# Experts' output rows scattered to their picks' places, and the combine stage regrouped, in a fused four-layer graph kernel

## The reference, cut to what matters

```python
x = _layernorm(x + _L3_gnn_ref(x, ...))          # x is [3125, 256], float32
# inside _L3_gnn_ref
x = m @ W_gc + b_gc + (feats @ W_res + b_res)    # "X4" in the kernel
vals, idx = top_k(x @ Wg + bg, 2); gates = softmax(vals)
h1 = gelu(rows_of_expert @ w1[e] + b1[e])        # 256 -> 512
h2 = h1 @ w2[e] + b2[e]                          # 512 -> 256
y = x + sum over the two picks of gate * h2[row]
out = (y - mean(y, 0)) * rsqrt(var(y, 0) + eps) * gamma + beta
```

## Time and profile before

| | |
|---|---|
| median of 3 runs | 2125.81 us (2124.03 to 2128.05) |
| the profiled execution's own time | 2125.8 us |
| its span | 2124.1 us |
| mean granted TensorE clock | 0.939 of full speed |
| busy share of the span | PE 86%, DVE 43%, ACT 22%, POOL 18% |
| moved by DMA | 553.6 MB, mean 261 GB/s |

### The profile page before, as it was taken

How to read it: one execution, slowest core, us unless ns; L and a number is a source line. 1 busy time by engine, 2 the same in 40 slices (tenths; PEclk the granted TensorE clock), 3 DMA queues, 4 the chain that set the end, 5 groups by cost and what they waited for, 6 DMA issues and landing times. The chain is left out here.

```text
span 2124.1 us, 34378 instructions
## 1 busy us (share of the span) xinstructions
PE 1819.4 (86%) x9586; PEld 1445.4 (68%) x9620; DVE 907.9 (43%) x2788; ACT 466.9 (22%) x1245; POOL 390.2 (18%) x723
## 2 busy tenths in 40 slices
PE   1988885999899899999989999899993999999451
PEld 0355554788688788777778878688882888888220
DVE  4976664444434411122211157736665121222256
ACT  0034444322222211111111111111110332232010
POOL 1022223311111200000000012214443111111451
PEclk8999997999999999999999999999996999999656
DMA  4178999999588688766668889889973999999421
GB/s 123 31 249 305 324 324 348 315 321 326 183 294 264 201 271 288 260 216 215 215 214 289 289 275 289 266 269 307 309 250 131 327 372 369 359 373 371 160 71 60
DMA packets 284900, 553.57 MB, mean 261 GB/s; under 512 B 17170, under 2 KB 208328, under 8 KB 281608
## 3 DMA queue, kind: packets, MB, share of 16 engines
q1 hardware_dynamic: 275976, 528.36, 75.1%
q0 software_dynamic: 8832, 24.13, 3.3%
HBM read 415.14 MB, written 137.29 MB: 260 GB/s over the span
## 5 line engine op out<-in xcount | busy, mean ns | idle before, releaser
L1001 PE MATMUL psum<-xsa,blk 128*128 128x512 f32 x2500 | 639.3, 405 | 18.1 <-DVEq L356 8.2
L1001 PEld LDWEIGHTS psum<-xsa,blk 128*128 128x128 f32 x2500 | 462.4, 191 | 106.5 <-issue 10.7
L1001 PE MATMUL psum<-xsb,blk 128*128 128x512 f32 (+1 forms) x1875 | 416.2, 369 | 6.0 <-DVEq L356 5.9
L1001 PEld LDWEIGHTS psum<-xsb,blk 128*128 128x128 f32 x1875 | 321.6, 190 | 64.8 <-issue 7.0
L1360 DVE TENSOR_SCALAR onehots<-counts_scratch 128x348 bf16<-128x348 f16 x464 | 161.6, 374 | 79.9 <-issue 41.5
L903 PE MATMUL psum<-onehots 128*128 128x349 bf16 x464 | 146.7, 316 | 40.8 <-DVE onehots L1365 38.5
L509 PE MATMUL psum<-route,expert_weights 128*128 128x128 f32 x1360 | 169.0, 278 | 0.0
L1759 POOL TENSOR_SCALAR ve<-mv 128x1 f32<-128x1 f32 x75 | 16.8, 223 | 820.5 <-DVE mv L1475 820.5
L906 PE MATMUL psum<-zrow 128*128 128x512 bf16 x431 | 160.8, 381 | 0.0
L509 PEld LDWEIGHTS psum<-route,expert_weights 128*128 128x128 f32 x1360 | 159.8, 193 | 0.9
L519 PE MATMUL psum<-expert_weights,route 128*128 128x256 f32 x672 | 159.1, 380 | 0.6 <-ACT route L568 0.6
(11 more groups left out here) (299 smaller groups left out, 2076.8 us busy)
## 6 DMA issues: line engine op xcount, KB each, us to landing
blk<-counts_src_on_rows SPq DMA_DIRECT2D x125, 832.0 KB, 4.7
blk<-counts_src_on_rows SPq DMA_DIRECT2D x125, 768.0 KB
expert_weights<-in_L_gnn_w SPq DMA_DIRECT2D x176, 512.0 KB, 6.1
blk<-counts_dst_on_rows SPq DMA_DIRECT2D x50, 832.0 KB, 4.5
counts_dst_on_rows<-band_rows SPq DMA_DIRECT2D x25, 1600.0 KB, 8.4
blk<-counts_dst_on_rows SPq DMA_DIRECT2D x50, 768.0 KB
counts_src_on_rows<-blk SPq DMA_DIRECT2D x13, 1600.0 KB, 8.6
counts_src_on_rows<-rblk SPq DMA_DIRECT2D x12, 1600.0 KB, 9.7
```

The lines of the kernel that those rows point to most:

```text
L1001: mm = e.matmul(o, blk[n][:, k * P:(k + 1) * P], XS[:, k, :, 0:Fw], start=(k == 0), stop=(k == T - 1 and not own))
```

## The change

`ids`, a new DRAM tensor with one number per slot, is filled with numbers past the last pick by SP early in the program. In l3, POOL scatters, beside each tile's rows, each pick's own number (2 x node + k) to the same slots of `ids`: two more indirect DMAs per tile. At the start of "experts" SP loads `ids`, PE turns it, and DVE casts it to `pick_of`, in which column c has the places of chunk c's 128 rows. POOL then copies a column and stores the chunk with an indirect DMA, row by row, to `ybuf` in the order of the picks; slots without a pick go to rows behind. Because of that order, five plain loads on SP bring all rows back, a group of five tiles each, behind the barrier. ACT multiplies them by the gates, DVE adds five tiles at a time and reduces them over the tiles, and PE has five sums to add up where it had 25 tiles. The squares are made and reduced in the same way. POOL adds beta to the residual, at the start of "experts". ACT applies the last layernorm's scale and shift. `ybuf` needs half as many zeroed rows.

```diff
 sync_moe:
+            e.dma_start(pick_rows[0:NCH, :], ids[0:NCH * P, :].rearrange("(c p) a -> c (p a)", p=P)).then_inc(S("inputs_loaded"), 16)
             for c in range(RING):
                 load_rows(c, c)
...
             phase_end(e, "experts")
+            for g in range(T // SPLIT):
+                lo, hi = g * SPLIT, (g + 1) * SPLIT
+                e.dma_start(picked_rows[:, lo:hi, :, :].rearrange("p t k f -> p t (k f)"),
+                            ybuf[TOP * lo * P:TOP * hi * P, :].rearrange("(t p k) f -> p t (k f)", t=SPLIT, p=P))\
+                    .then_inc(S(f"outs_in{g}"), 16)
 pe_moe:
+            e.wait_ge(S("inputs_loaded"), 16 * (LOADS + 2))
+            e.transpose(psum[:, 6, 0:P], pick_rows[:, :], identF[:, :]).then_inc(S("ids_turned"), 1)
             turn(0, 0, 0, 0)
...
-            for n, (name, buf) in enumerate((("combined", X4), ("squared", SQ))):
-                with e.Fori(0, T - 1) as t:
-                    e.wait_ge(S(name), t + 1)
-                    r = buf[:, bass.ds(t, 1), :].rearrange("p a f -> p (a f)")
-                    e.matmul(psum[:, n, 0:F], ones[:, :], r, start=False, stop=True, skip_group_check=True)
...
+            for n, (name, buf) in enumerate((("combined", sums_of), ("squares_added", squares_of))):
+                for g in range(T // SPLIT):
+                    e.wait_ge(S(name), g + 1)
+                    mm = e.matmul(psum[:, n, 0:F], ones[:, :], buf[:, g, :], start=(g == 0), stop=(g == T // SPLIT - 1))
+                mm.then_inc(S("bn_summed"), 1)
 act_moe:
-            tiles(e, square)
+            for t in range(T):
+                if t % SPLIT == 0:
+                    e.wait_ge(S(f"outs_in{t // SPLIT}"), 16)
+                for k in range(TOP):
+                    v = picked_rows[:, t, k, :]
+                    e.activation(v, v, ACT.Copy, scale=gate[:, k, t:t + 1]).then_inc(S("picks_scaled"), 1)
+            for g in range(T // SPLIT):
+                lo, hi = g * SPLIT, (g + 1) * SPLIT
+                e.wait_ge(S("centred"), g + 1)
+                if hi == T:
+                    hi -= 1
+                    e.activation(picked_rows[:, hi, 1, :], X4[:, hi, :], ACT.Square, scale=valid[:, hi:hi + 1])\
+                        .then_inc(S("squared"), 1)
+                e.activation(picked_rows[:, lo:hi, 1, :], X4[:, lo:hi, :], ACT.Square).then_inc(S("squared"), 1)
             phase_end(e, "combine")
+            for g in range(T // SPLIT):
+                e.wait_ge(S("out_shift"), g + 1)
+                for t in range(g * SPLIT, (g + 1) * SPLIT):
+                    e.activation(X4[:, t, :], X4[:, t, :], ACT.Identity, scale=out_r[:, t:t + 1], bias=out_shift[:, t:t + 1])\
+                        .then_inc(S("out_made"), 1)
 dve_moe:
-            st.done(e.tensor_scalar(slot_from[:, :, :], slot, 0.0, None, ALU.max))
+            st.done(e.tensor_scalar(X4[:, T - 1, :], X4[:, T - 1, :], valid[:, T - 1:T], None, ALU.mult))
+            e.wait_ge(S("ids_turned"), 1)
+            e.tensor_copy(pick_of[:, :], psum[:, 6, 0:P]).then_inc(S("picks_known"), 1)
...
-            for t in range(T):
-                r = ring[t % 4]
-                e.wait_ge(S(f"gathered{t % 4}"), 32 * (t // 4) + 32)
-                st.done(e.scalar_tensor_tensor(X4[:, t, :], r[:, 0, :], gate[:, 0, t:t + 1], X4[:, t, :], ...))
-                e.scalar_tensor_tensor(X4[:, t, :], r[:, 1, :], gate[:, 1, t:t + 1], X4[:, t, :], ...)
...
+            def over_tiles(v):
+                return v.rearrange("p t f -> p f t")
+            for g, b in enumerate(groups):
+                e.wait_ge(S("picks_scaled"), TOP * SPLIT * (g + 1))
+                y0, y1 = picked_rows[:, b, 0, :], picked_rows[:, b, 1, :]
+                st.done(e.tensor_tensor(y0, y0, y1, ALU.add))
+                st.done(e.tensor_tensor(X4[:, b, :], X4[:, b, :], y0, ALU.add))
+                e.tensor_reduce(sums_of[:, g, :], over_tiles(X4[:, b, :]), AX.X, ALU.add).then_inc(S("combined"), 1)
...
-            for t in range(T):
-                e.tensor_tensor(X4[:, t, :], X4[:, t, :], G[:, :], ALU.subtract).then_inc(S("centred"), 1)
+            def add_squares(g):
+                e.wait_ge(S("squared"), g + 1 + (g == len(groups) - 1))
+                e.tensor_reduce(squares_of[:, g, :], over_tiles(picked_rows[:, groups[g], 1, :]), AX.X, ALU.add)\
+                    .then_inc(S("squares_added"), 1)
+            for g, b in enumerate(groups):
+                e.tensor_tensor(X4[:, b, :], X4[:, b, :], G[:, :].unsqueeze(1).to_broadcast([P, SPLIT, F]), ALU.subtract)\
+                    .then_inc(S("centred"), 1)
+                if g:
+                    add_squares(g - 1)
+            e.wait_ge(S("centred"), len(groups))
+            add_squares(len(groups) - 1)
...
-                    for t in range((g - 1) * SPLIT, g * SPLIT):
-                        e.tensor_scalar(X4[:, t, :], X4[:, t, :], out_mv[:, t, 0:1], out_r[:, t:t + 1],
-                                        ALU.subtract, ALU.mult).then_inc(S("out_made"), 1)
 pool_moe:
-            e.wait_ge(S("rows_scattered"), 16 * TOP * T)
+            e.wait_ge(S("rows_scattered"), 2 * 16 * TOP * T)
             phase_end(e, "route")
+            for g in range(T // SPLIT):
+                b = slice(g * SPLIT, (g + 1) * SPLIT)
+                e.tensor_tensor(X[:, b, :], X[:, b, :], bc["bet"][:, :].unsqueeze(1).to_broadcast([P, SPLIT, F]), ALU.add)
+            e.wait_ge(S("picks_known"), 1)
...
+                    e.wait_ge(S(f"rows_stored{n}"), 16 * j)
+                    carry_wait(e)
+                    e.tensor_copy(pick_col[n][:, :], pick_of[:, bass.ds(c, 1)]).then_inc(S("pick_taken"), 1)
+                    e.wait_ge(S("pick_taken"), c + 1)
                     e.wait_ge(S("chunk_made"), c + 3)
-                    e.dma_start(ybuf[bass.ds(c * P, P), :], yout[n]).then_inc(S(f"rows_stored{n}"), 16)
+                    carry_wait(e)
+                    e.indirect_dma_start(out=ybuf, out_offset=bass.IndirectOffsetOnAxis(ap=pick_col[n][:, 0:1], axis=0),
+                                         in_=yout[n], in_offset=None).then_inc(S(f"rows_stored{n}"), 16)
...
-            for t in range(T):
-                if t >= 4:
-                    e.wait_ge(S("combined"), t - 3)
-                for k in range(TOP):
-                    e.indirect_dma_start(out=ring[t % 4][:, k, :], out_offset=None, in_=ybuf, ...)
...
+                e.tensor_scalar(out_shift[:, b], out_mv[:, b, 0], -1.0, None, ALU.mult).then_inc(S("out_eps"), 1)
+                e.tensor_tensor(out_shift[:, b], out_shift[:, b], out_r[:, b], ALU.mult).then_inc(S("out_shift"), 1)
 SP, behind "table":
+            e.dma_start(ids[0:NCH * P, :].rearrange("(p c) a -> p (c a)", p=P), pick_rows[:, 0:NCH])\
+                .then_inc(ld, 16)
 SP, zeroing of ybuf in l3:
-                            zero_rows(xbuf if ph == "l0" else ybuf, (2 * j + par - 2) * ZROWS, ZROWS)
+                            rows = ZROWS if ph == "l0" else YROWS
+                            zero_rows(xbuf if ph == "l0" else ybuf, (2 * j + par - 2) * rows, rows)
 l3_scatter, POOL:
                 for k in range(TOP):
                     e.indirect_dma_start(out=xbuf, out_offset=bass.IndirectOffsetOnAxis(ap=slot_to[:, k, i:i + 1], axis=0),
                                          in_=X4[:, i, :], in_offset=None).then_inc(S("rows_scattered"), 16)
+                    e.indirect_dma_start(out=ids, out_offset=bass.IndirectOffsetOnAxis(ap=slot_to[:, k, i:i + 1], axis=0),
+                                         in_=pick_id[:, k, i:i + 1], in_offset=None).then_inc(S("rows_scattered"), 16)
```

More of the change, by code:

```diff
@@ L30 @@
 FALL = 65536.0
+LOADS = 32
 PAGE_STEPS = 7
@@ L176, in gnn_program @@
         slot_to = sb("slot_to", [P, TOP, T], U32)
-        slot_from = sb("slot_from", [P, TOP, T], U32)
+        pick_id = sb("pick_id", [P, TOP, T])
+        pick_rows = sb("pick_rows", [P, P])
+        pick_of = sb("pick_of", [P, P], U32)
+        pick_col = [sb(f"pick_col{n}", [P, 1], U32) for n in range(RING)]
         def view(buf, at, n, dt):
@@ L290, in gnn_program @@
         assert at <= 10240
-        w1s, w2s, xin, xTs, hTs, yout, b2s, ring = ([] for _ in range(8))
+        w1s, w2s, xin, xTs, hTs, yout, b2s = ([] for _ in range(7))
         for base, lot, room in ((mw, ((w1s, (KF, H), RING), (w2s, (HT, F), RING)), T * PARTS * F * 2),
@@ L301, in gnn_program @@
             assert at <= room
[L302 to L311, removed]
+        picked_rows = mw[:, :].bitcast(F32).rearrange("p (t k f) -> p t k f", t=T, k=TOP)
+        at = 0
+        sums_of, at = cut(mx, at, (T // SPLIT, F))
+        squares_of, at = cut(mx, at, (T // SPLIT, F))
+        out_stats, at = cut(mx, at, (T, 6))
+        out_mv, at = cut(mx, at, (T, 2))
+        out_r, at = cut(mx, at, (T,))
+        out_shift, at = cut(mx, at, (T,))
+        bn_r, at = cut(mx, at, (KF,))
+        assert at <= 10240
```

(13 more changed lines are left out.)

68 lines of the change are left out of this document (26 added, 42 removed).

## The result

The changed kernel takes 2114.03 us (2107.64 to 2121.49, 13 runs); the kernel before, on the same chip, 2128.05 us (2122.61 to 2131.31, 13 runs). Ratio 0.9942, 95% interval 0.9928 to 0.9956: 0.6% faster, 13 us above the forecast of 2101 and 1 us outside the range.

A forecast was written before the change was run, and what follows sets the result against it. Experts were taken as bound by PE and DMA, combining by POOL's 50 gathers, the output stage by DVE. 2125.8 + 5.0 + 0.3 + 0 - 32.2 + 6.2 - 4.1 gave 2101 us, range 2086 to 2113.

The forecast's parts named there:

- Setup and route: Program setup and route stage: iotas and the ids store cost nothing, as they stand beside other work; dropping L605 gives -0.2 us.
- l3's end: End of l3: 50 more POOL scatters add 5.0 us, 2.5 over the last rounds and 2.5 for the last tile.
- the experts' start: Start of experts: the ids load delays the first rows by 0.5 us; start and route together +0.3 us.
- the combining: From the first DMA behind the experts to the mean: 40.0 us for 72.2, so -32.2 us.
- the centring: From the mean to the variance: 22.9 us, +6.2 us, as subtractions and reductions now stand in DVE's queue.
- the experts: Experts in steady state: the indirect store of each chunk changes nothing, 0 us, with chunks still at 3.85 us.
- Both rivals on this stage: Experts: row scatters at the gather's price, 2110.6 us, chance 0.19; chunk's store becomes the bound, 2159 us, chance 0.06.
- The barrier behind the experts falls when SP arrives at last: End of experts: SP's arrival opens the barrier, the last scatter being on its way some 11 us before; no cost.
- POOL ahead of SP as the last to arrive: Barrier behind the experts: a sign that would show the prediction wrong, POOL arriving last instead of SP.
- the rival of cheap reductions: Combining and centring: ten reductions at 1.5 us instead of 2.67, 11.7 us less, 2089 us; chance 0.10.
- Variance to output: From the variance to the output stage: the chain stays unchanged, 0 us.
- The output: Output stage up to the last scaled tile: 29.7 us against 33.8, so -4.1 us.

The follow-up runs named there:

- E3: The kernel before with the change's new SBUF buffers added but unused (1040 bytes a partition): 2138.52 us, ratio 1.0052.
- E17: The changed kernel with one unused buffer of 128 bytes a partition behind its own new buffers: 2099.71 us, ratio 0.9865.
- E5: The changed kernel with its small new buffers inside idle ones, so xsa and xsb start where they did before: 2102.35 us, ratio 0.9868.
- E7: The kernel before with only the ids scatters added in l3, no buffer moved: 2138.86 us, ratio 1.0048.
- E13: E5 with POOL's drain taken out of the barriers behind l3, route, the experts and the combining: 2087.62 us, ratio 0.9812.
- E14: The kernel before with POOL's drain taken out of the same four barriers as in E13, nothing else: 2113.72 us, ratio 0.9941.
- E10: E5 with POOL's drain taken out of the barriers behind l3, route and the experts: 2093.07 us, ratio 0.9837.
- E11: E5 with two more POOL drains, ahead of the scatters of tiles 8 and 16 of l3: 2101.82 us, ratio 0.9882.

## Why the prediction was wrong, and where it was right

**The step that failed** is a silence. "Setup and route. The iotas and the `ids` store stand beside loads and DVE's table work: nothing" counted the new instructions and not the new buffers, and the sum let the 1600 us ahead of the touched stages stand. The buffers moved `xsa` and `xsb` by 1152 bytes, and each of the matmuls that fill h1a, h2a and h2b took 2.6% longer. In E3 that is 11.4 us in the median and 14.2 us from the first aggregate to the last (1228.9 for 1214.7 us); in the changed kernel, by E17's and E5's ratio against the first one's (0.9865 and 0.9868 for 0.9942), 15.7 to 16.4 us. With that healed the time is 2099.7 and 2102.4 us for the forecast 2101. That it comes so near is in part luck: in the table, l3's end (+5.6 against the forecast) and the experts' start (+1.0) are made up for by the combining, the centring, the step to the output and the experts. The sign was right, and none of the rivals came.

**l3's end was undersized** by 5.6 us. The tail was nearly right: from the last aggregate to the end of the last scatter 35.9 us for 31.5, +4.3 against 5.0. What the step left out stands behind it. The words "the other engines enter "route" on POOL's arrival" took the stretch from POOL's last issue to the barrier as fixed. It was 4.2 us and became 10.4, though the DMA queues moved nothing in the last 9 of these. E7 shows that the scatters alone do it. E13 and E14 show what of it is the drain's: with no drains, the way from the last aggregate to the first chunk is 55.5 and 46.3 us, 9.2 for the extra scatters, where it is 64.3 (E5) and 52.0 (before) with them, 12.3. So 3 us of the excess are the longer drain. The rest is there without drains too. Then the barrier behind route opens when the scatters have landed, in E13 6.3 us behind the end of the last one (1638.23), in E14 1.5 us behind it (1633.67). The first row past that barrier, in E13, then in E14:

```profile
1644.56 0.35 DVE L643 TENSOR_SCALAR X<-X,valid 128x256 f32<-128x256 f32 x1 [6.84 <-POOLq L363]
```
```profile
1635.17 0.35 SPq L436 DMA_DIRECT2D route<-expert_rows_in  x1
```

The semaphore's events say the same in every trace: the last one of `rows_scattered` comes 6.3 to 7.2 us behind the end of the last scatter in the ten traces with the `ids` scatters, E7's among them, and 1.4 to 1.5 us behind it in the ten without, though the last packet has ended 0.8 and 1.1 us behind it. So of the barrier's 6.2 us more, 4.8 are the later landing and the other 1.4 the drain, which ends 4.2 us behind the landing instead of 2.7. Whether it is the four bytes a row that land late, or four scatters a tile instead of two, was not tried. Behind the barrier the `ids` load and its turning add some 1.5 us: the first turned rows reach VectorE 4.2 us after it in E13 (at 1648.79) and 2.8 us after it in E14 (at 1637.93).

**The experts** cost nothing, as forecast. The -3.4 us is mostly the spread of executions: first to last chunk takes 318.6 to 323.8 us in the eleven profiles of kernels with the old store (mean 321.5), and 319.1 to 320.9 in the nine with the new one (mean 319.9). At most 1.6 us are a gain. q0's packets stayed at 48 a chunk (2452 in 200 us, 8.4% for the earlier trace rows's 8.8%). Both rivals on this stage fall. What the prediction read at its end was wrong, at no cost: "The barrier behind the experts falls when SP arrives at last". In E14, with POOL's drains out and nothing else changed, the first gather comes 7.4 us after the last chunk (1969.78), where in the kernel before it was 14.3 us:

```profile
1977.20 1.02 POOL L710 DMA_INDIRECT expert_weights<-expert_rows_out,slot_from  x1 [5.80 <-SPq L360]
```

So POOL's drain held that barrier in the kernel before, whatever names, and it holds it in the changed one, as E10 shows: the sign "POOL ahead of SP as the last to arrive" came, but was no sign of the change.

**Combining** came out at 38.6 us for 40.0, with DVE without a gap from 2027.54 on, as described. A group took 5.3 us and not 5.7, since the reduction over tiles costs 2.26 us at pace (2.35 busy) and not 2.67: 1.8 ns an element for L1409's 2.09. It is nearer to that row than to a sum of 1280 neighbours (1.49), so the rival of cheap reductions falls too. The rule of the Trainium skill, "VectorE: DVE Perf Modes", section "Mode 1× (REGULAR) — the baseline", that strides are taken as they come, at one result per cycle, does not agree with 2.35 us for 1280 strided elements against the 1.49 of a sum of as many neighbours; a reduction of 1280 neighbours was not timed.

**The centring** took 20.1 us for 22.9: the five reductions at 0.4 us less each are 2 of the 2.8. **Variance to output** was forecast as unchanged and fell by 1.8 us: what stood before L672 was POOL's drain behind the gathers (2.52 us, POOLq), and there are no gathers now. E14 shows it: with the drains out and the gathers there, the stretch is 4.5 us, where it was 6.3. It is the one place where the same oversight worked for the change. **The output** came to 30.1 us for 29.7.

**What stays open.** Why 128 bytes past a multiple of 256 is the fast start: the runs show a rule for this 128x512 fp32r moving operand and its 128x128 weights in `blk`, which kept its place; other shapes and other places of `blk` were not tried, and the buffers that lie behind `xsa` (`X4`, `route`, `expert_weights`) moved along with it each time. And what a drain of POOL waits for. It is not the queues' traffic, which had ceased, and it is more than the landing: at the end of l3 it ends 4.2 us behind the last landing in the five traces with 100 indirect DMAs before it, 2.7 to 2.8 us in those with 50, 1.5 us in E11 with 36. The number alone does not explain it: 32 of them cost 3.2 us in mid-stage, where the last had landed (at 1499.65) before POOL came to the drain, and 36 cost 8.4 at the end, 6.8 of them until the landing.

## What to carry to other kernels

When a change adds a buffer, ask what it pushes. If an operand that fills TensorE's time moves, look at the number of matmuls in an equal window of an untouched stage; if it fell at the same clock, put 128 bytes of room ahead of it and time that before judging the change. Two aggregates of the trace, one early and one late, cost nothing to compare and would have put this loss in view at once.

A drain of POOL behind indirect DMAs is work on the critical path, and taking out one alone proves little, since the next one pays. Where semaphores already cover what POOL wrote and sent, take out all of them: 15 us of 2100 here, in either kernel. E13, with both remedies, is the fastest kernel of this study, 1.9% under the one before.

## What the runs showed of the hardware that was not expected

- A matmul with a 128x512 fp32r moving operand: 225.7 ns with the operand's start 128 bytes past a multiple of 256, 228.3 at 192, 231.5 at 0, PE always busy and the clock full. The Trainium skill, "SBUF — State Buffer", section "Operand start alignment", names only the element's size as a rule and says of it that this is about legality, not speed; the runs agree as to legality and show the speed.
- POOL's sequencer runs ahead of the issues in its timeline (where the profile's spans are rough). With the drain out, the barrier behind l3 opened at 1634.30 us in E13 (DVE's L624), before the last scatter's issue shows at all:

```profile
1634.30 0.23 DVE L624 TENSOR_TENSOR route<-route,iota_e 128x64 f32<-128x64 f32 x1 [3.44 <-POOLq L363]
...
1637.28 0.95 POOL L1839 DMA_INDIRECT pick_of_row<-pick_id,slot_to  x1 [0.30 <-issue]
```

- A landing can be signalled long after the last packet: 6.3 to 7.2 us behind the issue's end for the last `ids` scatter, with packets ended after 0.8 us; 1.4 to 1.5 us for scatters of 1 KB rows alone, with packets ended after 1.1 us.
- An fp32 reduction of 1280 elements with a step of 1 KB costs VectorE 2.35 us; a sum over two operands of 1280 neighbours, 1.49.
